# Attention block on one core: the far tiles of the transposed probabilities turned by VectorE in 32x32 blocks and put together by sixteen transfers a unit

## The chip, the cores and the metric

The kernel runs on one core of a Trainium2 chip. The metric is the time of one execution on the device in microseconds (us). The engines are TensorE (PE in the profile, its weight loads PEld), VectorE (DVE), ScalarE (ACT), GpSimd (POOL) and SyncE (SP), which here only issues DMA transfers. SBUF is the on-chip memory, PSUM the memory that TensorE writes its products to. Each engine works through its own queue in order; semaphores order the engines among each other.

## The reference

Two attention layers with layer norms between them and a mixture of experts at the end, for 2 batches of 1024 rows of 256. The part that the change touches is the second attention, 16 heads of 128:

```python
q = q * cos + _rotate_half(q) * sin
k = k * cos + _rotate_half(k) * sin
scores = jnp.einsum('bhqd,bhkd->bhqk', q, k) / math.sqrt(HD)
scores = jnp.where(causal[None, None], scores, jnp.finfo(jnp.float32).min)
probs = jax.nn.softmax(scores.astype(jnp.float32), axis=-1).astype(q.dtype)
out = jnp.einsum('bhqk,bhkd->bhqd', probs, v)
out = out.transpose(0, 2, 1, 3).reshape(b, s, H * HD)
return out @ wo + bo
```

## The kernel before

The work is cut into 34 units: units 0 and 1 are the first attention of the two batches, units 2 to 33 one head of one batch each (`unit_of`; a pair of heads is four units, and `r` in the code is the unit's place in its pair). The 1024 rows of a unit are 8 tiles of 128 queries. Every product is done three times, with operands split into a high part (fp32r) and a low part (the rest): ScalarE writes the high part (`high_...`), VectorE or GpSimd subtracts it (`low_...`), and `product` on TensorE multiplies high by high, high by low and low by high.

For a unit u the steps are: `project_q(u, x)` for x = 0 to 3 (queries and keys of 512 rows each); `add_bias` (ScalarE), `swap` (SP, two transfers of 128 KB that exchange the halves of 64 partitions), `rotate` (VectorE), `turn` (GpSimd, two operations), `high_qk`, `low_qk` (GpSimd); `scores(u, i)` for tile i, its causal width (i + 1) x 128; `row_max` (VectorE, which also adds the mask); `exponent` (ScalarE, into `prob_s` for tiles 0 to 3 and into the two halves of `prob_b` in turn for tiles 4 to 7); `transposes(u, i)` on TensorE, one for each 128 keys, through two PSUM banks `ps_t`; `high_p` and `low_p`, which write the transposed probabilities as `pT_hi` and `pT_lo`; `outputs(u, c)` for the 512 queries of half c; `high_o`, `low_o`; `out_project(u, c, g)`; and `accumulate` on VectorE. `project_v` makes the values of a pair of heads, half of them in each unit.

For tiles 4 to 7 the transposes come in two groups (`TG`): 4 far tiles (keys 0 to 511, all of them visible) and i - 3 near tiles (keys 512 to 1023, up to the diagonal). A unit has 10 transposes for tiles 0 to 3 and 16 far and 10 near ones for tiles 4 to 7.

The order is written out by hand, as one list for each engine, `head(u)`, in the middle of which n = u + 1 stands for the next unit: its projections and rotations are done beside the exponents of unit u. `head` runs for u = 3 to 30; `start` and `ends` hold the orders of the first and the last units. The products on TensorE that aren't scores or transposes take the two banks `ps_m` in turn (`take_bank`): a product waits until the contents of the bank from two uses before have been read. `work` (`qb`, `qs`, `qc`) holds the queries and keys on their way through the rotation, `rows` and `hf` are used by the layer norms alone.

## Time and profile before

| | us |
|---|---|
| runs before, median of 3 (lowest to highest) | 1116.94 (1116.71 to 1118.32) |
| profiled execution, from the first to the last instruction | 1115.4 |
| TensorE busy | 1105.2 |
| VectorE busy | 834.9 |
| ScalarE busy | 748.3 |
| GpSimd busy | 638.1 |
| queue of SP, share of the 16 DMA engines' span | 19.9% |

The profiled execution's span leaves out what lies around the first and last instruction. TensorE's busy time is the union of its records, and its records overlap. A row of a timeline gives the start and the length of an instruction; where an engine works without a gap, the distance from one start to the next is what an instruction costs it.

### The profile page before, as it was taken

The numbers are of one execution on the slowest core, as the hardware profiler recorded it, in microseconds if no ns is written. First come the engines' busy times: TensorE is split into PE (matmuls) and PEld (weight loads), VectorE is DVE, ScalarE is ACT, GpSimd is POOL, SyncE is SP. The second block draws the span as 40 slices with busy tenths as digits, with TensorE's granted clock in tenths as the row PEclk, the third lists the DMA queues.
The fourth block names the chain that finished last, engine by engine and source line by source line (L and its number), as shares of the span: only waits on it lengthen the run. The fifth ranks groups of instructions, "written<-read, shape, count | busy, mean of one in ns | idle before, by whom it ended". The sixth has DMA issues, their size and how long they took to land.

```text
span 1115.4 us, 20396 instructions
## 1 busy us (share of the span) xinstructions
PE 1105.2 (99%) x7100; PEld 1006.7 (90%) x7100; DVE 834.9 (75%) x1978; ACT 748.3 (67%) x1584; POOL 638.1 (57%) x516
## 2 busy tenths in 40 slices
PE   9999999999999999999999999999999999999997
PEld 8999899999999999999999999999999999988897
DVE  7776777777777777777777777777777777977776
ACT  5666867666666666666666666666666666688765
POOL 2217666555555555555555555555555556777676
PEclk9999999999999999999999999999999999999999
DMA  5002412121212121212121212121211212230102
GB/s 176 1 1 62 129 39 53 39 62 39 52 39 62 39 53 39 60 39 50 37 60 39 52 39 62 39 48 44 62 38 37 50 40 57 48 110 14 39 1 76
DMA packets 33285, 56.54 MB, mean 51 GB/s; under 512 B 5792, under 2 KB 10016, under 8 KB 33184
## 3 DMA queue, kind: packets, MB, share of 16 engines
q1 hardware_dynamic: 33040, 55.21, 19.9%
q8 instruction: 57, 0.93, 0.3%
q14 instruction: 44, 0.36, 0.1%
q10 hardware_dynamic: 144, 0.03, 0.0%
HBM read 17.47 MB, written 4.19 MB: 19 GB/s over the span
## 4 chain that ended last, share of the span: by engine, by line
PE 95%; POOL 2%; issue 1%; ACT 1%; DMA 1%; DVE 1%; SPq 0%; POOLq 0%; ACTq 0%; DVEq 0%
PE ps_m L458 58%; PE ps_s L458 23%; PE ps_t L608 12%; PE ps_m L505 1%; DMA work<-in_attn_w 0%; POOL acc L2341 0%; POOL qk_lo L2346 0%; PE ps_m L479 0%; POOL wqk_lo L2346 0%; PE ps_t L458 0%; POOL pT_lo L2354 0%; DMA work<-work 0%; POOL acc L2330 0%; PE ps_m L666 0%; PE ps_m L667 0%
## 5 line engine op out<-in xcount | busy, mean ns | idle before, releaser
L2296 POOL TENSOR_TENSOR work<-work,rope 128x512 f32<-128x512 f32 x128 | 165.5, 1293 | 222.8 <-DMA work<-work 222.7
L1784 DVE TENSOR_TENSOR pT_lo<-ps_t,pT_hi 128x512 fp32r<-128x512 f32 (+3 forms) x408 | 210.8, 551 | 32.7 <-ACT pT_hi L1201 30.2
L1201 ACT ACTIVATE pT_hi<-ps_t 128x512 fp32r<-128x512 f32 (+3 forms) x408 | 182.8, 489 | 65.3 <-PE ps_t L608 65.1
L1777 DVE CUSTOM_DVE_ANT_0 ps_s<-ps_s,causal 128x128 f32<-128x128 f32 (+7 forms) x272 | 203.5, 767 | 6.7 <-PE ps_s L458 4.1
L2300 POOL TENSOR_TENSOR work<-work 128x512 f32<-128x512 f32 x128 | 167.6, 1310 | 10.0
L2307 POOL TENSOR_TENSOR qk_lo<-work,qk_hi 128x512 fp32r<-128x512 f32 x128 | 163.0, 1293 | 17.8 <-ACT qk_hi L1158 17.8
L1152 ACT ACTIVATE work<-ps_m,bqk 128x512 f32<-128x512 f32 x128 | 88.8, 694 | 116.5 <-PE ps_m L458 116.4
L1817 DVE SCALAR_TENSOR_TENSOR acc<-ps_m,rinv,acc 128x256 f32<-128x256 f32 x272 | 118.6, 478 | 63.0 <-PE ps_m L458 61.7
L1194 ACT ACTIVATE prob_b<-ps_s,nmax 128x640 f32<-128x640 f32 (+3 forms) x136 | 130.3, 958 | 17.9 <-DVE nmax L1777 14.6
L458 PE MATMUL ps_s<-qk_hi 128*128 128x384 f32 (+5 forms) x384 | 140.6, 366 | 0.0
L1738 DVE SCALAR_TENSOR_TENSOR work<-ps_m,bqk,rope 128x512 f32<-128x512 f32 x128 | 95.5, 746 | 54.3 <-ACT work L1152 54.0
L458 PE MATMUL ps_m<-pT_lo,v_hi 128*128 128x512 f32 (+3 forms) x384 | 132.6, 345 | 0.0
L458 PE MATMUL ps_m<-pT_hi,v_lo 128*128 128x512 f32 (+3 forms) x384 | 132.6, 345 | 0.0
L458 PE MATMUL ps_s<-qk_lo,qk_hi 128*128 128x384 f32 (+5 forms) x384 | 131.5, 343 | 0.0
L458 PE MATMUL ps_s<-qk_hi,qk_lo 128*128 128x384 f32 (+5 forms) x384 | 130.9, 341 | 0.0
L458 PE MATMUL ps_m<-pT_hi,v_hi 128*128 128x512 f32 (+3 forms) x384 | 130.1, 339 | 0.0
L608 PE MATMUL ps_t<-ident,prob_b 128*128 128x128 f32 x884 | 120.1, 274 | 0.4 <-DVE pT_lo L1784 0.4
L608 PEld LDWEIGHTS ps_t<-ident,prob_b 128*128 128x128 f32 x884 | 99.7, 140 | 9.8 <-issue 1.2
L458 PE MATMUL ps_m<-hT_hi,wqk_hi 128*128 128x512 f32 x256 | 103.6, 405 | 0.0
L1158 ACT ACTIVATE qk_hi<-work 128x512 fp32r<-128x512 f32 x128 | 79.1, 641 | 36.4 <-POOL work L2300 36.3
L458 PE MATMUL ps_m<-hT_lo,wqk_hi 128*128 128x512 f32 x256 | 101.0, 395 | 0.0
L458 PE MATMUL ps_m<-hT_hi,wqk_lo 128*128 128x512 f32 x256 | 100.5, 393 | 0.0
(235 smaller groups left out, 2822.7 us busy)
## 6 DMA issues: line engine op xcount, KB each, us to landing
work<-work SPq DMA_DIRECT2D x256, 128.0 KB, 2.3
wst<-in_head_qk SPq DMA_DIRECT2D x16, 256.0 KB, 2.9
acc<-in_x_tiles SPq DMA_DIRECT2D x8, 256.0 KB, 6.8
wo_st<-in_L_ffn_wo SPq DMA_DIRECT2D x16, 128.0 KB, 2.4
wst<-in_pair_v SPq DMA_DIRECT2D x8, 256.0 KB, 3.0
x_rows<-acc SPq DMA_DIRECT2D x4, 512.0 KB, 3.6
wst<-in_expert SPq DMA_DIRECT2D x8, 256.0 KB, 3.0
rope<-x_rows SPq DMA_DIRECT2D x4, 512.0 KB, 4.1
```

The lines of the kernel that those rows point to most:

```text
L458: ins = pe.matmul(out, lhs[x], rhs[y], start=first and k == 0, stop=last and k == 2)
L608: last = pe.transpose(t_bank(u, i, j)[:, k * P:(k + 1) * P], probs(i)[:, part], ident[:, :])
L1152: act.activation(qb[:, x % 2, :], m_bank("q", u, x), ACT.Identity, bias=bqk[:, j, head_:head_ + 1]).then_inc(qb_done.sem, qb_done.up(u, x))
L1194: act.activation(probs(i), all_scores[:, score_range(i)], ACT.Exp, bias=nmax[:, u % 2, i:i + 1], scale=-1.0, accum_out=rsum[:, u % 2, i:i ...
L1201: act.activation(pT_hi[:, slots, cols], t_bank(u, i, j)[:, 0:size * P].rearrange("p (j q) -> p j q", q=P), ACT.Copy).then_inc(t_hi.sem, t_ ...
L1738: dve.scalar_tensor_tensor(qc[:, ring3(u, x), :], m_bank("q", u, x), bqk[:, j, head_:head_ + 1], cos_t[:, c * CH:(c + 1) * CH], ALU.add, A ...
L1777: dve.tensor_tensor_reduce(s, s, causal[:, T - (i + 1) * P:T], -1.0, ABOVE_ALL, ALU.add, ALU.min, accum_out=nmax[:, u % 2, i:i + 1]).then_ ...
L1784: dve.tensor_tensor(pT_lo[:, slots, cols], t_bank(u, i, j)[:, 0:size * P].rearrange("p (j q) -> p j q", q=P), pT_hi[:, slots, cols].bitcas ...
L1817: last = dve.scalar_tensor_tensor(acc[:, b, tile, :], src[:, t * D:(t + 1) * D], rinv[:, u % 2, tile:tile + 1], acc[:, b, tile, :], ALU.mu ...
L2296: pool.tensor_tensor(qs[:, x % 2, :], qs[:, x % 2, :], sin_t[:, c * CH:(c + 1) * CH], ALU.mult).then_inc(sin_done.sem, sin_done.up(u, x))
L2300: pool.tensor_tensor(qc[:, ring3(u, x), :], qc[:, ring3(u, x), :], qs[:, x % 2, :], ALU.add).then_inc(rope_done.sem, rope_done.up(u, x))
L2307: pool.tensor_tensor(qk_lo[:, u % 2, j, cols], qc[:, ring3(u, x), :], qk_hi[:, u % 2, j, cols].bitcast(F32), ALU.subtract).then_inc(qk_lo_ ...
```

## The change

For the units 3 to 30 (`FAR_UNITS`) the 16 far transposes leave TensorE. VectorE turns each tile's 512 far keys in blocks of 32x32 into a buffer `turned` (`turn_far`, four operations a unit). It takes the place of `rows` and `hf`. A block transpose leaves every block in its own 32 partitions; so sixteen transfers of 32 partitions x 512 elements, 64 KB each, put the blocks where the product needs them: `exchange(u)` on SP issues 8 of them and `exchange(u)` on ScalarE the other 8, each once the fourth `turn_far` is done and the near product of the first half has been read out of `pT`. They land in the slots 0 to 3 of `pT_lo`, keys in order. `high_far` (ScalarE) then rounds two slots' worth at a time into `pT_hi`, `low_far` (VectorE) subtracts it in place, both from SBUF to SBUF with 1024 columns in an operation, two a unit. Since the queries of a tile come in four groups of 32 that way, the near tiles are written in the same order of queries (`by_quarter`), and `high_o` and `low_o` put them back. `outputs(u, 1)` becomes `near_outputs(u)` and two times `far_outputs(u, k)`, near first, with the columns and the number of products as before. `exponent` waits in addition for `turn_far` on the half of `prob_b` that it writes over, and `turn_far(u, 4)` for both queues' transfers of the unit before.

```diff
+FAR_UNITS = range(3, LAST - 2)
+FAR = 4 * CH
+Q4 = 32
...
+def groups_of(u, i):
+
+    return [(1, i - 3)] if is_far(u) and i >= 4 else list(enumerate(TG[i]))
...
-        rows = sb("rows", [P, TC, D])
-        hf = sb("hf", [P, KD, CH])
+        shared_ln = sb("shared_ln", [P, FAR])
+        rows = shared_ln[:, 0:TC * D].rearrange("p (t d) -> p t d", d=D)
+        hf = shared_ln[:, TC * D:FAR].rearrange("p (k n) -> p k n", n=CH)
+        turned = shared_ln[:, :].rearrange("p (g m i q) -> p g m i q", g=4, m=4, i=4)
+        turned_by_keys = shared_ln[:, :].rearrange("p (g n) -> p g n", g=4)
...
+            def far_outputs(u, k):
...
+                pe.wait_ge(far_lo.sem, far_lo.at(u, k))
...
+                for j in (2 * k, 2 * k + 1):
+                    high, low = (x[:, 0:4, j * P:(j + 1) * P] for x in (pT_hi, pT_lo))
+                    last = product(out, (v_hi[:, s, j, vals], v_lo[:, s, j, vals]), (high, low), False, j == TC - 1)
...
+            def high_far(u, k):
+                act.wait_ge(exchanged.sem, exchanged.at(u))
+                act.wait_ge(exchanged_act.sem, exchanged_act.at(u))
+                act.activation(far_part(pT_hi, k), far_part(pT_lo, k).bitcast(F32),
+                               ACT.Copy).then_inc(far_hi.sem, far_hi.up(u, k))
+
+            def exchange(u):
+                act.wait_ge(turn_done.sem, turn_done.at(u, NT - 1))
+                act.wait_ge(pv_mm.sem, pv_mm.at(u, 0))
+                for g in (2, 3):
+                    for k in range(4):
+                        act.dma_start(pT_lo[k * Q4:(k + 1) * Q4, g, :].bitcast(F32),
+                                     turned_by_keys[g * Q4:(g + 1) * Q4, k, :]).then_inc(exchanged_act.sem, 16)
+                exchanged_act.up(u)
...
+            def turn_far(u, i):
+                dve.wait_ge(exp_done.sem, exp_done.at(u, i))
...
+                dve.transpose(out=turned[:, :, :, i - 4, :].rearrange("p g m q -> p m g q"),
+                              in_=prob_b[:, i % 2, 0:CH].rearrange("p (m g k) -> p m g k", g=4, k=Q4)).then_inc(turn_done.sem, turn_done.up(u, i))
+
+            def low_far(u, k):
+                dve.wait_ge(far_hi.sem, far_hi.at(u, k))
+                dve.tensor_tensor(far_part(pT_lo, k), far_part(pT_lo, k).bitcast(F32), far_part(pT_hi, k).bitcast(F32),
+                                  ALU.subtract).then_inc(far_lo.sem, far_lo.up(u, k))
...
                 swap(n, 1)
+                exchange(u)
                 swap(n, 2)
```

The lists of `head(u)` are written in another order. TensorE's new list in full:

```
T(u,0) T(u,1) project_q(n,0) out_project(u-1,1,0) T(u,2) T(u,3) scores(u,4) scores(u,5)
project_q(n,1) out_project(u-1,1,1) T(u,4) scores(u,6) scores(u,7) outputs(u,0) T(u,5)
project_q(n,2) project_q(n,3) T(u,6) T(u,7) out_project(u,0,0) scores(n,0) scores(n,1)
scores(n,2) out_project(u,0,1) project_v project_v scores(n,3) near_outputs(u)
far_outputs(u,0) far_outputs(u,1)                         (T is transposes)
```

The three engines whose order the prediction speaks of, first ScalarE, from the second half of a unit to the first exponents of the next. `pT_hi<-ps_t` is a copy of transposed probabilities, `work<-ps_m` is add_bias, `prob_s` and `prob_b` are exponents. Before:

```order
L1194 ACTIVATE prob_b,rsum<-ps_s,nmax 128x1024 [waits t_mm,max_done]
L1201 ACTIVATE pT_hi<-ps_t 128x4x128 [waits t_mm]
L1201 ACTIVATE pT_hi<-ps_t 128x3x128 [waits t_mm]
L1163 ACTIVATE v_hi<-ps_m 128x512 [waits v_mm]
L1201 ACTIVATE pT_hi<-ps_t 128x4x128 [waits t_mm] x2
```

and now:

```order
L1269 ACTIVATE pT_hi<-ps_t 128x12x32 [waits t_mm]
L1218 ACTIVATE work<-ps_m,bqk 128x512 [waits swapped_1,qk_mm]
L1269 ACTIVATE pT_hi<-ps_t 128x16x32 [waits t_mm]
L1283 DMA pT_lo<-shared_ln 32x512 [waits pv_mm,turn_done]
L1283 DMA pT_lo<-shared_ln 32x512 x7
L1229 ACTIVATE v_hi<-ps_m 128x512 [waits v_mm]
L1275 ACTIVATE pT_hi<-pT_lo 128x4x256 [waits exchanged_act,exchanged] x2
L1263 ACTIVATE prob_s,rsum<-ps_s,nmax 128x128 [waits t_mm,max_done]
```

Behind the last near copies stand the eight issues, then the values, and then the two large copies that wait for both queues' transfers; the next unit's exponents moved behind those.

VectorE, in the middle of a unit, around the low part of the first half's output (`oT_lo`). Before:

```order
L1777 ISA ps_s,nmax<-ps_s,causal 128x896 [waits s_mm]
L1777 ISA nmax 128x1
L1795 RECIPROCAL rinv<-rsum 128x4 [waits exp_done]
L1790 TENSOR_TENSOR oT_lo<-ps_m,oT_hi 128x512 [waits o_hi]
L1784 TENSOR_TENSOR pT_lo<-ps_t,pT_hi 128x4x128 [waits t_hi]
```

and now:

```order
L1861 ISA ps_s,nmax<-ps_s,causal 128x1024 [waits s_mm]
L1861 ISA nmax 128x1
L1878 STREAM_TRANSPOSE shared_ln<-prob_b 128x4x4x32 [waits exp_done]
L1888 TENSOR_TENSOR oT_lo<-ps_m,oT_hi 128x512 [waits o_hi]
L1878 STREAM_TRANSPOSE shared_ln<-prob_b 128x4x4x32 [waits exp_done]
L1867 TENSOR_TENSOR pT_lo<-ps_t,pT_hi 128x8x32 [waits t_hi]
```

The first transpose there is tile 6, the second tile 7; `oT_lo`, on which project_q(n, 3) waits for its bank, stands behind the row maximum of tile 7 and the transpose of tile 6. Before, it stood right behind the row maximum of tile 6.

TensorE, at the end of a unit: the second half's product, whose first row is a far tile and which ends with the near tiles of 512, 384, 256 and 128 columns; two steps of three are left out. Before:

```order
L458 MATMUL ps_m<-pT_hi,v_hi 128x512 [waits t_lo,v_lo_done]
...
L458 MATMUL ps_m<-pT_hi,v_hi 128x512 [waits t_lo]
...
L458 MATMUL ps_m<-pT_hi,v_hi 128x384
...
L458 MATMUL ps_m<-pT_hi,v_hi 128x256
...
L458 MATMUL ps_m<-pT_hi,v_hi 128x128
```

and now:

```order
L499 MATMUL ps_m<-pT_hi,v_hi 128x512 [waits t_lo,v_lo_done]
...
L499 MATMUL ps_m<-pT_hi,v_hi 128x4x96
...
L499 MATMUL ps_m<-pT_hi,v_hi 128x4x64
...
L499 MATMUL ps_m<-pT_hi,v_hi 128x4x32
...
L499 MATMUL ps_m<-pT_hi,v_hi 128x512 [waits far_lo]
...
L499 MATMUL ps_m<-pT_hi,v_hi 128x512 [waits far_lo]
...
L649 MATMUL ps_t<-ident,prob_s 128x128 [waits t_lo,exp_done] x2
```

The near product comes first now, and each half of the far product waits for its own `low_far`.

## Rows read from the trace of the kernel before

**Rows 1.** The page: busy time of each engine, and the chain that ended last

```profile
PE 1105.2 (99%) x7100; PEld 1006.7 (90%) x7100; DVE 834.9 (75%) x1978; ACT 748.3 (67%) x1584; POOL 638.1 (57%) x516
...
PE 95%; POOL 2%; issue 1%; ACT 1%; DMA 1%; DVE 1%; SPq 0%; POOLq 0%; ACTq 0%; DVEq 0%
```

**Rows 2.** Busy time by stretch of eight units; then TensorE's clock, DMA share, GB/s

```profile
core 0: us, PE busy (x) PEld busy (x) DVE busy (x) ACT busy (x) POOL busy (x), PEclk, DMA share, GB/s
278.42:504.65 226.23, 226.21 (x1442) 206.23 (x1441) 169.01 (x377) 149.87 (x331) 128.54 (x103) 1.00 0.21 47
504.65:730.71 226.06, 226.06 (x1442) 206.35 (x1441) 169.30 (x377) 149.87 (x331) 128.54 (x103) 1.00 0.21 48
```

**Rows 3.** Timeline of TensorE: start us, length us, engine, line, operation, tiles

```profile
503.05 1.03 PE L608 MATMUL ps_t<-ident,prob_b 128*128 128x128 f32 x8
...
503.84 0.38 PE L458 MATMUL ps_m<-wv_hi,hT_hi 128*128 128x256 f32 x1
...
506.06 0.40 PE L458 MATMUL ps_m<-pT_hi,v_hi 128*128 128x512 f32 x1
506.29 0.39 PE L458 MATMUL ps_m<-pT_lo,v_hi 128*128 128x512 f32 x1
...
511.12 0.42 PE L458 MATMUL ps_s<-qk_hi 128*128 128x384 f32 x1
...
511.38 0.33 PE L458 MATMUL ps_s<-qk_lo,qk_hi 128*128 128x384 f32 x1
511.55 0.34 PE L458 MATMUL ps_s<-qk_hi,qk_lo 128*128 128x384 f32 x1
```

**Rows 4.** Groups by line and shape, ScalarE and VectorE: busy us, mean ns; a timeline pair

```profile
L1201 ACT ACTIVATE pT_hi<-ps_t 128x512 fp32r<-128x512 f32 x171 | 98.6, 595 | 28.5 <-PE ps_t L608 28.5
L1030 ACT ACTIVATE acc<-acc 128x1024 f32<-128x1024 f32 x1 | 1.1, 1078 | 0.0
...
L1784 DVE TENSOR_TENSOR pT_lo<-ps_t,pT_hi 128x512 fp32r<-128x512 f32 x170 | 114.2, 685 | 23.1 <-ACT pT_hi L1201 23.1
L1777 DVE CUSTOM_DVE_ANT_0 ps_s<-ps_s,causal 128x1024 f32<-128x1024 f32 x29 | 35.5, 1223 | 0.0
L1624 DVE CAST hT_hi<-hf 128x256 fp32r<-128x256 f32 x2 | 0.6, 288 | 0.0
...
557.76 0.98 ACT L1201 ACTIVATE pT_hi<-ps_t 128x512 fp32r<-128x512 f32 x2 [0.18 <-PE ps_t L608]
558.62 0.60 ACT L1163 ACTIVATE v_hi<-ps_m 128x512 fp32r<-128x512 f32 x1
```

**Rows 5.** DMA issues (timeline; us to landing by form) and what a swap moved

```profile
0.74 0.41 ACTq L1025 DMA_DIRECT2D vec<-in_vectors  x1
...
0.74 0.39 SPq L2520 DMA_DIRECT2D acc<-in_x_tiles  x1
1.18 0.42 SPq L2523 DMA_DIRECT2D work<-in_attn_w  x1
...
231.74 0.46 SPq L2555 DMA_DIRECT2D work<-work  x1
232.25 0.59 SPq L2556 DMA_DIRECT2D work<-work  x1
232.89 0.58 SPq L2535 DMA_DIRECT2D wst<-in_head_qk  x1
233.51 0.45 SPq L2540 DMA_DIRECT2D wst<-in_pair_v  x1
...
work<-work SPq DMA_DIRECT2D x256, 128.0 KB, 2.3
wst<-in_head_qk SPq DMA_DIRECT2D x16, 256.0 KB, 2.9
out_rows<-prob_b SPq DMA_DIRECT2D x2, 128.0 KB, 1.7
...
501.00:501.50 0.50, 0.50 (x7) 0.50 (x6) 0.24 (x2) 0.33 (x3) 0.50 (x1) 1.00 0.94 197
501.50:502.00 0.50, 0.50 (x6) 0.50 (x5) 0.03 (x1) 0.50 (x2) 0.41 (x1) 1.00 1.02 221
```

**Rows 6.** Timeline: VectorE's operation with both inputs in SBUF, and GpSimd beside it

```profile
227.04 0.66 DVE L1751 SCALAR_TENSOR_TENSOR wqk_lo<-wst,wqk_hi 128x512 fp32r<-128x512 f32 x1
...
517.78 1.29 POOL L2296 TENSOR_TENSOR work<-work,rope 128x512 f32<-128x512 f32 x1
518.13 1.48 DVE L1751 SCALAR_TENSOR_TENSOR wqk_lo<-wst,wqk_hi 128x512 fp32r<-128x512 f32 x1
519.14 1.62 POOL L2300 TENSOR_TENSOR work<-work 128x512 f32<-128x512 f32 x1
```

200 lines of the change are left out of this document (130 added, 70 removed).

## The prediction

> **What bounds the kernel now.** Three views in this order. First the table of busy time and the chain that ended last [rows 1]: TensorE is busy 1105.2 of 1115.4 us and carries 95% of the chain, VectorE 75%, ScalarE 67%, GpSimd 57%. Then the busy times of a stretch of eight units [rows 2]: 226.23 us, 28.28 us a unit (the next eight 226.06, 28.26), TensorE without a gap at full clock, VectorE 21.1 and ScalarE 18.7 us a unit. The 28 units from 3 to 30, which the change touches, are 28 x 28.26 = 791 us of the span. So only TensorE's own work counts there today, and nothing that another engine does until it makes TensorE wait. Third the timelines of the engines around a unit, for prices and for the order in which things wait.
>
> TensorE's prices are distances between starts, since its records overlap. Eight transposes start at 503.05 and the next product at 503.84: 0.10 us each, although a record lasts 0.27. Products of 512 columns start 0.23 apart [rows 3].
>
> **Taken away on TensorE.** Of the 36 transposes of a unit the 16 far ones go: 1.6 us. Where a product follows transposes its first step is stretched by about 0.1 (0.26 instead of 0.17 us for 384 columns, [rows 3]); eight such places become five, 0.3 us. The products keep their columns. TensorE's own work falls from 28.26 to about 26.4 us a unit; all of it over 28 units would be 53 us.
>
> **Moved to others.** VectorE loses four subtractions of 512 columns from PSUM (0.69 each, [rows 4]), and gets four block transposes of 512 and two subtractions of 1024 columns with both inputs in SBUF. No transpose of VectorE is in the trace. Below stands the conversion of 256 columns at 0.29, which doubled is some 0.45; above the two-input operation held up to 1.48 us [rows 6]; I take the 0.69 of the plain 512-column form, as it reads and writes as many columns. The 1024-column subtractions I put at 1.2, like the row maximum of 1024 [rows 4]. VectorE comes to 21.1 - 2.7 + 2.8 + 2.4 = 23.6 us a unit. ScalarE loses four copies of 512 (0.60), gets two of 1024 (1.08, [rows 4]) and eight DMA issues: 18.7 - 2.4 + 2.2 + 4.5 = 23.0. SP issued eight DMAs a unit and mostly waited; it now issues sixteen. None of the three reaches 26.4 by its sum, so the question is the chain of one exchange.
>
> **The price of an issue.** A single swap issue on SP lasts 0.46 us, one right behind it 0.59, and four in a row start at 231.74, 232.25, 232.89 and 233.51, 0.59 apart; the first ones of the kernel start 0.47 apart, and the one issue on ScalarE lasts 0.41 [rows 5]. The eighth issue thus starts 3.3 to 4.4 us behind the first; I take 3.9 (0.56 apart), between the short and the long spacing. ScalarE can do nothing else for some 4.5 us. A swap's two transfers moved 197 to 221 GB/s while in flight [rows 5], so 64 KB is 0.3 us of transfer: issuing, not moving, sets the pace. The Trainium skill (DMA: Bandwidth & Descriptors, Issuing engines are not separate DMA queues) says that issuing from several engines only saves sequencer time, usually small beside the transfer. By the rows it is larger; were it small, as that page has it, the sum below would shrink by about 1.5 us a unit. That is the first rival.
>
> **The sum for one unit,** from the first transpose on TensorE (0). Up to the end of the near product `outputs(u, 0)` TensorE has 23,040 columns (10.25 us at 0.23 per 512), 11 transposes and three changes: 11.7. project_q(n, 3) needs the bank that this product leaves, so the high part (0.2 + 0.60 on ScalarE) and the low part (0.69 on VectorE, behind row_max(u, 7) and turn_far(u, 6)); it starts at 13.6 instead of 13.4 and ends at 15.0. The three transposes of tile 6 end at 15.4. ScalarE does high_p(u, 6), add_bias(n, 3) and high_p(u, 7) behind them, starts 0.43 to 0.6 apart [rows 4], and issues its first transfer at **17.1**. SP, which waits for the last block transpose alone, starts about 14.5 and is done first, so ScalarE's half decides: the last issue at 21.0 (+3.9); landed at 23.2 (+2.2: the swaps' median from issue to landing is 2.3 for 128 KB, [rows 5]; 1.7 is the shortest of any form there, 2.9 to 3.0 that of loads of 256 KB); high_far(u, 0) done at 24.3 (+1.1); low_far(u, 0) at 26.0 (+1.2, and +0.5 for the wait below); low_far(u, 1) at 27.7 (the same again), while TensorE finishes the first far product; the second far product 1.4: **29.1**.
>
> The 0.5: the trace has one operation of VectorE with both inputs in SBUF in the units, L1751. It lasts 0.66 with GpSimd idle and 1.48 at 518.13, where GpSimd is in an operation from 517.78 and the next one, begun at 519.14, is itself stretched to 1.62 [rows 6]. So the two hold each other. low_far is such an operation, and at that time GpSimd is in its densest stretch, six operations of 1.29 us for (n, 2) and (n, 3), whose swaps SP now issues behind the exchange. The wait is 0 to 1.3 for each of the two; I take 0.5, somewhat under the mean of 0.65.
>
> What TensorE has meanwhile: from 15.4 the last transposes, out_project, scores, project_v and near_outputs, about 7.9 us with the waits for banks, so it stands from about 23.5 to 26.1 and again for a moment ahead of the second far product. The late ScalarE work, exponent(n, 3) and high_o(u, 1), delays out_project(u, 1, 0) in the next unit by 0 to 0.3 us; I leave it at 0.
>
> Result: 29.1 - 28.26 = +0.84 us a unit, over 28 units +23.5 us. The profiled execution is 1115.4 us from first to last instruction, the median of three runs 1116.94, 1.5 us more, and that holds for both kernels: 1116.9 + 23.5 = **1140 us**. The units outside 3 to 30 keep their order.
>
> **Bounds.** Cheapest: the exchange starts at 16.6, issues 3.3, landing 1.7, no wait for GpSimd, block transposes at 0.45: 16.6 + 3.3 + 1.7 + 1.1 + 1.2 + 2.8 = 26.7, near TensorE's own 26.4. Dearest: 17.9 (block transposes of 1.3) + 4.4 + 3.2 + 1.1 + 2.5 + 2.5 + 1.4 = 33.0. Neither end has all its terms at once with much chance.
>
> **Rivals.**
> (A) Faster: issuing on ScalarE is cheap. Place: exchange(u) in ScalarE's queue. The gain and loss meet where 29.1 becomes 28.26, so at seven spacings of 0.44 instead of 0.56. If ScalarE's sequencer issues while its last copies still run (exchange at 16.6) and at 0.42 a piece, as its only row has it, the unit is 16.6 + 2.9 + 2.2 + 1.1 + 1.7 + 1.7 + 1.4 = 27.6: -18 us, 1098. For it: that row of 0.41. Against it: every string of issues in the trace. 0.20. The same with no wait for GpSimd and everything hidden, 26.4 to 26.7 us a unit, 1064 to 1073: 0.05.
> (B) The gains and the new wait cancel within 0.2%, 28.18 to 28.34 us a unit: 0.05.
> (C) Slower by more: GpSimd takes the port between the two low_far each time. Then the second starts 1.3 us late and not 0.5, the first up to 1.3 too: 29.1 + 1.6 = 30.7, +68 us, 1185. For it: GpSimd's next operation did follow at once at 519.14. Partly so, +0.8 us a unit, would be 1163. 0.15 together.
> (D) The two queues hinder each other: ScalarE's issues run into SP's last ones and into the swaps (n, 2) and (n, 3) behind them, some six issues of 0.5 us; waiting for them adds up to 3 us: 32, 1220. Against it: at 0.74 us both queues started an issue together, and each took its 0.4 us [rows 5]. The Trainium skill (Perfetto Trace Analysis, DMA Instruction — HWDGE) says the opposite, that the descriptor generator is shared by the sequencers and locked while one uses it; by the rows nothing is added. 0.05.
> The change does what it says: the order on the engines shows the 16 transposes gone and the sixteen transfers there.
>
> **Chances.** Forecast (28.34 to 30.0 us a unit) 0.50, A 0.25 in all, B 0.05, C 0.15, D 0.05. The range from 1095 to 1178 holds the forecast, B, A without its far end and the partial C. A measurement of this kernel can tell about 0.2% (2.2 us) from no change: faster 0.25, same 0.05, slower 0.70.
>
> **What would show it.** In the changed profile: units of 29.1 us; TensorE's busy share down and its longest waits on pT_lo of low_far; eight issues on ScalarE 0.56 apart from 17.1 in the unit, landing about 2.2 behind the last; low_far of 1.2 to 2.5 us beside GpSimd. I am wrong if TensorE stays near 99% (A), if the wait ahead of the far products is mainly on GpSimd's account (C), or if issues on either queue last over 1 us (D). A block transpose of much over 0.7 us would move the wait to project_q(n, 3).

## The result and the profile after the change

The changed kernel takes **1279.2 us** (median; 1276.5 to 1286.9), the kernel before 1117.6 in the same comparison: a ratio of 1.146, 95% interval 1.142 to 1.149. The forecast was 1140 with a range up to 1178: the sign was right, the size was not. The difference of 162 us is 5.8 us for each of the 28 units, where 0.84 was forecast.

The page of the changed kernel, its busy times and its chain, stands against [rows 1]: TensorE falls from 1105.2 us in a span of 1115.4 to 1133.4 in 1279.1, and from 95% of the chain to 51%. VectorE (19%), ScalarE's DMA queue (ACTq, 10%), DMA (7%) and ScalarE come in.

```profile
span 1279.1 us, 20088 instructions
...
PE 1133.4 (89%) x6652; PEld 981.6 (77%) x6652; DVE 955.4 (75%) x2034; ACT 734.9 (57%) x1528; POOL 688.7 (54%) x516
...
PE 51%; DVE 19%; ACTq 10%; DMA 7%; ACT 6%; issue 5%; POOL 2%; SPq 0%; POOLq 0%; DVEq 0%
```

The busy times of eight units (columns as in [rows 2]) show where to look: 270.60 us, 33.8 a unit instead of 28.26, TensorE without work for 35.8 us of them, 4.5 a unit, and a granted clock of 0.94 instead of 1.00. Its busy time, 234.78, is no less than the 226.21 of before, though 16 transposes a unit are gone: where the clock falls, the same products take longer. (How much, the run with all three changes shows below.)

```profile
core 0: us, PE busy (x) PEld busy (x) DVE busy (x) ACT busy (x) POOL busy (x), PEclk, DMA share, GB/s
311.30:581.90 270.60, 234.78 (x1314) 200.46 (x1313) 201.50 (x392) 145.76 (x313) 142.50 (x103) 0.94 0.30 71
```

The list of what TensorE waits for (total us, times, longest) names three places: low_far (L1883), the exponents (prob_b), and the low part of the values (v_lo), which frees the bank that the near product writes.

```profile
PE ps_m L499 <- DVE pT_lo L1883: 60.7, 43, 2.3
PE ps_t L649 <- ACT prob_b L1263: 32.5, 14, 3.3
PE ps_m L499 <- DVE v_lo L1829: 27.5, 28, 2.1
```

**One unit followed along its chain** (an r = 2 unit; its first transpose on TensorE is at 581.88). ScalarE's timeline: the first of its eight issues is at 599.10, 17.2 us in, 17.1 was forecast. The eight last until 604.13, and high_far starts at 606.28.

```profile
598.99 0.68 ACT L1218 ACTIVATE work<-ps_m,bqk 128x512 f32<-128x512 f32 x1
599.10 0.52 ACTq L1283 DMA_DIRECT2D pT_lo<-shared_ln  x1
599.56 0.60 ACT L1269 ACTIVATE pT_hi<-ps_t 128x512 fp32r<-128x512 f32 x1
599.65 4.48 ACTq L1283 DMA_DIRECT2D pT_lo<-shared_ln  x7
604.18 0.60 ACT L1229 ACTIVATE v_hi<-ps_m 128x512 fp32r<-128x512 f32 x1 [4.02 <-issue]
606.28 2.00 ACT L1275 ACTIVATE pT_hi<-pT_lo 128x1024 fp32r<-128x1024 f32 x2 [1.50 <-DMA pT_lo<-shared_ln]
```

VectorE: the last block transpose takes 0.71 (0.69 was forecast); both low_far together 4.09, and GpSimd's two operations beside them 2.15 and 2.27 instead of 1.29 (first fence VectorE, second GpSimd).

```profile
596.70 0.71 DVE L1878 STREAM_TRANSPOSE shared_ln<-prob_b 128x512 f32<-128x512 f32 x1 [0.18 <-ACT prob_b L1263]
...
607.37 4.09 DVE L1883 TENSOR_TENSOR pT_lo<-pT_lo,pT_hi 128x1024 fp32r<-128x1024 f32 x2 [1.87 <-ACT pT_hi L1275]
```
```profile
606.86 1.29 POOL L2400 TENSOR_TENSOR work<-work,rope 128x512 f32<-128x512 f32 x1 [7.46 <-DMA work<-work]
608.23 2.15 POOL L2404 TENSOR_TENSOR work<-work 128x512 f32<-128x512 f32 x1
610.34 2.27 POOL L2400 TENSOR_TENSOR work<-work,rope 128x512 f32<-128x512 f32 x1
```

On TensorE the near product ends at 607.7; the far products wait for low_far:

```profile
609.28 0.50 PE L499 MATMUL ps_m<-pT_hi,v_hi 128*128 128x512 f32 x1 [1.60 <-DVE pT_lo L1883]
611.52 0.50 PE L499 MATMUL ps_m<-pT_hi,v_hi 128*128 128x512 f32 x1 [0.57 <-DVE pT_lo L1883]
```

The next unit begins at 613.01. This unit lasts 31.1 us, so the forecast's chain is the right one and 2.0 us short in it: 0.1 up to the first issue, 1.1 from there to high_far, 0.7 in the two low_far, the rest behind them.

**The next unit, r = 3, is another matter.** From the timelines of ScalarE and, in the last row, TensorE:

```profile
615.54 0.64 ACT L1236 ACTIVATE wqk_hi<-wst 128x512 fp32r<-128x512 f32 x1
620.97 0.42 ACT L1251 ACTIVATE wo_hi<-wo_st 128x256 fp32r<-128x256 f32 x1 [4.79 <-PE ps_m L499]
621.30 0.96 ACT L1269 ACTIVATE pT_hi<-ps_t 128x384 fp32r<-128x384 f32 x2
623.19 0.79 ACT L1263 ACTIVATE prob_b<-ps_s,nmax 128x640 f32<-128x640 f32 x1 [0.93 <-DVE nmax L1861]
...
624.13 0.33 PE L649 MATMUL ps_t<-ident,prob_b 128*128 128x128 f32 x1 [3.25 <-ACT prob_b L1263]
```

high_o_weights (L1251) stands 4.79 us for the last product of `out_project(u - 1, 1, 1)`, which reads the weights that it overwrites, and high_p(u, 2), high_p(u, 3) and exponent(u, 4) stand behind it in ScalarE's queue. TensorE then stands 3.25 us ahead of `transposes(u, 4)`. The changed order had put that step at the unit's start; before, it stood at the end. The other half of the weights, `high_o_weights(p, 1)` in the r = 0 units, kept its place, but exponent(u, 4) moved behind it. In the kernel before, the r = 3 copy waited for nothing and the r = 0 copy up to 1.4 us, 9.8 us in all; in the changed kernel both wait, 56.1 us in 14 times. From the timeline of before:

```profile
335.36 0.42 ACT L1185 ACTIVATE wo_hi<-wo_st 128x256 fp32r<-128x256 f32 x1
347.52 0.42 ACT L1185 ACTIVATE wo_hi<-wo_st 128x256 fp32r<-128x256 f32 x1 [1.40 <-PE ps_m L458]
```

The prediction does not speak of these steps.

Over all 28 units, from the timelines of TensorE, ScalarE and VectorE, the chain's terms are (means, in us; the columns on the right are kernels from the experiments below):

| term | forecast | changed | both weight steps late | and swap(n, 2) first | and swap(n, 3) inside |
|---|---|---|---|---|---|
| first transpose to ScalarE's first issue | 17.1 | 18.31 | 16.59 | 16.60 | 16.36 |
| first issue to start of high_far | 6.1 | 8.25 | 8.14 | 7.45 | 8.13 |
| high_far to low_far | 1.1 | 1.09 | 1.09 | 1.09 | 1.09 |
| the two low_far | 3.4 | 4.22 | 4.24 | 3.64 | 2.36 |
| end of low_far to the next unit | 1.4 | 2.16 | 2.07 | 1.75 | 2.00 |
| unit | 29.1 | 34.02 | 32.14 | 30.54 | 29.95 |
| time of the kernel | 1140 | 1279.2 | 1225.5 | 1177.6 | 1166.6 |

### The profile page after: what moved, and what is told of

It reads as the page before. It is cut to its first block, busy times and chain, and to the rows that moved or that the text cites. A ratio compares the mean times of both kernels' runs of the same rounds, so it can differ in the third digit from the quotient of the medians.

```text
span 1279.1 us, 20088 instructions
## 1 busy us (share of the span) xinstructions
PE 1133.4 (89%) x6652; PEld 981.6 (77%) x6652; DVE 955.4 (75%) x2034; ACT 734.9 (57%) x1528; POOL 688.7 (54%) x516
## 4 chain that ended last, share of the span: by engine, by line
PE 51%; DVE 19%; ACTq 10%; DMA 7%; ACT 6%; issue 5%; POOL 2%; SPq 0%; POOLq 0%; DVEq 0%
PE ps_m L499 32%; PE ps_s L499 12%; ACTq L1283 10%; DVE pT_lo L1883 7%; DMA pT_lo<-shared_ln 6%; PE ps_t L649 5%; DVE ps_s L1861 4%; ACT pT_hi L1275 2%; DVE shared_ln L1878 2%; ACT pT_hi L1269 2%; DVE acc L1915 1%; DVE pT_lo L1867 1%; DVE work L1822 1%; DVE oT_lo L1888 1%; DVE wqk_lo L1835 1%
## 5 line engine op out<-in xcount | busy, mean ns | idle before, releaser
L2400 POOL TENSOR_TENSOR work<-work,rope 128x512 f32<-128x512 f32 x128 | 193.0, 1508 | 338.5 <-DMA work<-work 338.5
L499 PE MATMUL ps_m<-pT_hi,v_hi 128*128 128x512 f32 (+3 forms) x384 | 150.6, 392 | 93.2 <-DVE pT_lo L1883 60.7
L2404 POOL TENSOR_TENSOR work<-work 128x512 f32<-128x512 f32 x128 | 189.4, 1480 | 10.0
L1867 DVE TENSOR_TENSOR pT_lo<-ps_t,pT_hi 128x512 fp32r<-128x512 f32 (+3 forms) x296 | 142.7, 492 | 58.0 <-ACT pT_hi L1269 57.8
L499 PEld LDWEIGHTS ps_m<-pT_hi,v_hi 128*128 128x128 f32 x384 | 78.9, 205 | 134.1 <-DVE pT_lo L1883 74.6
L1883 DVE TENSOR_TENSOR pT_lo<-pT_lo,pT_hi 128x1024 fp32r<-128x1024 f32 x56 | 118.1, 2147 | 59.6 <-ACT pT_hi L1275 59.6
L1269 ACT ACTIVATE pT_hi<-ps_t 128x512 fp32r<-128x512 f32 (+3 forms) x296 | 125.3, 451 | 39.7 <-PE ps_t L649 39.4
L499 PE MATMUL ps_m<-pT_lo,v_hi 128*128 128x512 f32 (+3 forms) x384 | 143.2, 373 | 0.0
L1229 ACT ACTIVATE v_hi<-ps_m 128x512 fp32r<-128x512 f32 x72 | 42.9, 596 | 143.8 <-PE ps_m L499 82.4
L1263 ACT ACTIVATE prob_s<-ps_s,nmax 128x128 f32<-128x128 f32 (+3 forms) x136 | 70.9, 524 | 66.8 <-DVE nmax L1861 66.6
```

Of the source, the lines that this page charges most:

```text
L499: ins = pe.matmul(out, lhs[x], rhs[y], start=first and k == 0, stop=last and k == 2)
L1263: act.activation(probs(i), all_scores[:, score_range(i)], ACT.Exp, bias=nmax[:, u % 2, i:i + 1], scale=-1.0, accum_out=rsum[:, u % 2, i:i ...
L1269: act.activation(transposed(pT_hi, u, i, j), t_tiles(u, i, j), ACT.Copy).then_inc(t_hi.sem, t_hi.up(u, i, j))
L1867: dve.tensor_tensor(transposed(pT_lo, u, i, j), t_tiles(u, i, j), transposed(pT_hi, u, i, j).bitcast(F32), ALU.subtract).then_inc(t_lo.sem ...
L1883: dve.tensor_tensor(far_part(pT_lo, k), far_part(pT_lo, k).bitcast(F32), far_part(pT_hi, k).bitcast(F32), ALU.subtract).then_inc(far_lo.se ...
L2400: pool.tensor_tensor(qs[:, x % 2, :], qs[:, x % 2, :], sin_t[:, c * CH:(c + 1) * CH], ALU.mult).then_inc(sin_done.sem, sin_done.up(u, x))
```

## Experiments

Times are medians; the kernel before gave 1116.6 to 1117.0 beside all of them.

### The weight steps on ScalarE

```diff
                 if r == 3:
                     high_qk_weights(p + 1, 1)
-                    high_o_weights(p + 1, 0)
                 high_p(u, 2)
 ...
                 high_p(u, 4)
+                if r == 3:
+                    high_o_weights(p + 1, 0)
                 exponent(u, 6)
```

> One step moved: on ScalarE high_o_weights(p + 1, 0) goes from ahead of high_p(u, 2) to behind high_p(u, 4); nothing is left out. In the trace of the changed kernel ScalarE stands 4.8 us ahead of the first half of this step in each of the 7 units that have it (56.1 us in 14 waits on out_project's last product), and high_p(u, 2) and high_p(u, 3) stand behind it; TensorE waits up to 3.3 us for them and later for prob_b (32.5 us in all), and the units with this step last some 37 us, those behind them 34, the others 31 to 33. Theory W (the moved weight step costs on its own): the 7 long units fall to the length of the others, 4 to 7 us each, so 1279 - 28 to 49 = 1230 to 1251. Rival E (the exchange's chain sets each unit, the stall only takes its place): at most 1 us a unit, 1272 to 1279.

Measured: 1240.1, ratio 1.109 (1.106 to 1.112). Theory W: 39 us from the place of one copy. ScalarE's first issue in the seven r = 3 units comes at 16.4 us on the mean instead of 20.9. In the r = 0 units it stays at 19.1, and ScalarE's waits still show a wait of that step, 24.7 us in 7 times; that is the other half of the weights, `high_o_weights(p, 1)`. So that was moved as well:

```diff
-                if r == 0:
-                    high_o_weights(p, 1)
                 exponent(u, 4)
 ...
                 high_p(u, 4)
+                if r == 0:
+                    high_o_weights(p, 1)
```

> Both steps on the output weights stand behind high_p(u, 4) on ScalarE: high_o_weights(p + 1, 0) of the r = 3 units and high_o_weights(p, 1) of the r = 0 units (the kernel of 1240 had moved the first alone). Nothing is left out. In the changed kernel's trace ScalarE's first issue comes 16.0 and 17.1 us behind the unit's first transpose in r = 1 and r = 2 units, 20 to 22 in r = 3 and 19.2 in r = 0; with the first step late the r = 0 units stay at 19.0. Theory W (the second step is the same stall): the r = 0 units come to 16.0 to 16.5, 2.5 to 3 us in each of 7: 1240 - 21 = 1219, 1212 to 1225. Rival V (the r = 0 units are late through add_value_bias(p, 1) on VectorE): 1236 to 1244.

Measured: 1225.5, ratio 1.097 (1.095 to 1.099), 15 us less where 21 were expected, at the upper end of theory W: the mechanism holds (ScalarE no longer waits ahead of L1251, the first issue comes at 16.59 on the mean), the gain is somewhat smaller. Together the two steps cost 54 us.

### The number of transfers

```diff
-                    for k in range(4):
+                    for k in (0,):
                         act.dma_start(pT_lo[k * Q4:(k + 1) * Q4, g, :].bitcast(F32),
```
(and the same on SP)

> Leaves out 12 of the 16 transfers of each exchange, so that three quarters of the far tiles are old data: SP issues 2 and ScalarE 2. Everything else, the waits too, is as in the changed kernel. Theory I (the string of issues sets the chain): ScalarE's last issue comes 6 x 0.65 = 3.9 us sooner, and the landing behind it, 2.7 in the trace, falls to 2.0 or so; 3.9 to 4.5 us a unit while the chain is late, down to TensorE's own 26.4: 33.7 - 4.5 = 29.2, 28 x 4.5 = 126, so 1153 to 1170, with the stall of the weight step still in it. Rival P (a fixed time from the first issue to the landing, or the order of the steps, holds the units): less than 1.5 us a unit, 1237 or above. Rival Q (the queues hinder each other, so that fewer transfers free SP too): more than 5 us a unit, under 1140.

Measured: 1171.4, ratio 1.048 (1.047 to 1.050): 108 us less, 3.9 a unit. Theory I, 1.4 us above its range: from the first issue to high_far it takes 4.8 us instead of 8.2. TensorE's waits show low_far almost gone (4.3 us instead of 60.7), those on v_lo down (10.2 instead of 27.5) and the wait of the weight step untouched (32.1); the granted clock is 0.984 instead of 0.964. So the 108 us are what the late chain cost in all above TensorE's own work and the waits of the weight steps, not the price of twelve issues by themselves.

### GpSimd beside low_far

```diff
+                w_ = 16 if is_far(u - 1) else CH
-                pool.tensor_tensor(qs[:, x % 2, :], qs[:, x % 2, :], sin_t[:, c * CH:(c + 1) * CH],
+                pool.tensor_tensor(qs[:, x % 2, 0:w_], qs[:, x % 2, 0:w_], sin_t[:, c * CH:c * CH + w_],
```
(and so in the other two steps)

> GpSimd's three steps of the rotation (L2398 to L2404 and the subtraction behind it) work on 16 columns instead of 512 in the units behind a unit with an exchange; the rest of their columns is left out. VectorE and all waits stay. In the trace of the changed kernel the two low_far last 2.15 us each while GpSimd works, 4.1 to 4.6 for both, and GpSimd's operations beside them 2.15 to 2.27 instead of 1.5. Theory G (the two engines hold each other): low_far falls to 1.2 each, 2 us a unit, and the rotation ends sooner: 1279 - 28 x 2 = 1223, 1210 to 1235. Rival V (a subtraction with both inputs in SBUF in this form lasts 2.1 by itself): low_far stays at 2.0 to 2.2 and the time within 1265 to 1279.

Measured: 1206.7, ratio 1.081 (1.078 to 1.084): 72 us less, more than theory G asked for. The rows of low_far, first in the changed kernel, then here (shortest, median and longest in ns):

```profile
L1883 DVE TENSOR_TENSOR pT_lo<-pT_lo,pT_hi x56: 1337/2294/2325, 170.5 to 1087.4; 128x1024 fp32r<-128x1024 f32 x56
```
```profile
L1883 DVE TENSOR_TENSOR pT_lo<-pT_lo,pT_hi x56: 1215/1226/1242, 168.0 to 1019.5; 128x1024 fp32r<-128x1024 f32 x56
```

All 56 last 1.22 to 1.24 with GpSimd nearly idle, the 1.2 of the sum; beside GpSimd 46 of the 56 last 2.2 to 2.3. Rival V is out. The hold itself is 52 us of the 72 (28 x 1.84, from 4.22 for the pair to 2.38). The rest is spread: by the timelines 0.3 us a unit ahead of the first issue, 0.1 from there to high_far and 0.2 behind low_far, at a clock of 0.984 instead of 0.964. What makes the first part is not shown; GpSimd's rotation ends sooner there too.

### Do the costs add, and what is TensorE's own work?

> The late weight step and the small GpSimd steps together (GpSimd's rotation works on 16 of 512 columns in the units behind an exchange; the rest is left out). Alone they gave 1240 and 1207, 39 and 72 us under the changed kernel. Theory S (two separate costs on the path of different units or places): they add, 1279 - 39 - 72 = 1168; 1158 to 1178. Rival T (they overlap): 1185 to 1205. What is left above 1117 is then the exchange's chain with the forecast's own prices: issue, landing, high_far, low_far 1.23, second far product.

Measured: 1175.1, ratio 1.051 (1.049 to 1.054): 104 of the 111 us that the two gave apart. They add nearly.

> The late weight step, the small GpSimd steps, and 4 of 16 transfers, together (12 transfers and most of GpSimd's rotation are left out). Sum of the three savings: 39 + 108 + 72 = 219, 1060. Theory F (TensorE's own work is 26.4 us a unit, as forecast): the units can't become shorter than 26.4, so 1117 - 28 x 1.86 = 1065 at best, 1065 to 1085. Rival O (the order of the steps has waits of its own): units above 27.5, over 1095.

Measured: 1096.9, ratio 0.982 (0.981 to 0.984), above theory F and at the lower edge of rival O. The three gave 219 us apart and 182 together. The units last 27.6 us on the mean. A stretch of 226 us there has TensorE busy for 221.10 (columns as above):

```profile
400.00:626.00 226.00, 221.10 (x1345) 195.97 (x1344) 190.91 (x404) 150.37 (x323) 31.16 (x106) 1.00 0.23 57
```

So its own work is 27.6 x 0.978 = 27.0 us a unit, near the 26.4 of the forecast, and the order has 0.6 us of small waits besides; the second weight step is still among them (24.4 us of ScalarE's waits, 9.4 of TensorE's on prob_b). Own work of 27.0 would have been worth 28 x 1.26 = 35 us, not 53, and this run, with most of the exchange and the rotation left out, gets 20 of them.

It also gives a size to the fall of the clock. From the start of the second exchange unit to the end of the last, 27 units, TensorE is busy in the changed kernel and here (first row and second):

```profile
175.68:1096.47 920.79, 789.80 (x4436) 671.47 (x4434) 688.91 (x1326) 494.77 (x1065) 485.17 (x347) 0.95 0.29 70
170.70:916.32 745.62, 727.82 (x4435) 645.72 (x4434) 625.22 (x1326) 493.70 (x1063) 97.20 (x346) 1.00 0.24 58
```

That is 29.3 and 27.0 us a unit for the same products: of the 6.5 us by which the units differ, 2.3 are products that take longer, and 4.2 are TensorE without work. How much of the 2.3 lies on the chain and how much beside it is not separated.

### The order of the change with the transposes back on TensorE

```diff
-FAR_UNITS = range(3, LAST - 2)
+FAR_UNITS = range(0)
 ...
-                transposes(u, 4)
                 scores(u, 6)
                 scores(u, 7)
                 outputs(u, 0)
+                transposes(u, 4)
                 transposes(u, 5)
```
(the block transposes, the exchange, high_far and low_far go; on ScalarE high_qk(n, 0) and high_o(u, 0), on VectorE row_max(u, 7) and low_o(u, 0) stand ahead of high_p(u, 4) and low_p(u, 4))

> The changed kernel's order of steps on all engines, but the far tiles are transposed by TensorE as before, without block transposes, exchange, high_far and low_far; transposes(u, 4) stands behind outputs(u, 0), since it writes what that product reads. Nothing is left out. Theory O1 (order harmless except for the weight step): TensorE has its 28.26 us a unit again and stands only in the units with the weight step, 3 to 7 us in each of 7: 1117 + 21 to 49 = 1138 to 1166. Rival O2 (the order itself, with exponent(u, 4) late and the late rotations, makes TensorE wait in each unit): over 1 us more a unit, 1180 to 1230. Rival O3 (the weight step's stall comes only together with the exchange): 1117 to 1130.

Measured: 1273.7, ratio 1.140 (1.139 to 1.142), worse than any theory had it. Its waits say why, and that it is no clean test:

```profile
PE ps_t L649 <- DVE pT_lo L1862: 76.2, 57, 1.5
PE ps_s L499 <- ACT prob_b L1261: 32.1, 14, 3.3
PE ps_m L499 <- DVE v_lo L1824: 10.5, 7, 2.1
```

The second row is the weight step. The first is new: with all transposes in it, `transposes(u, 4)` to `transposes(u, 7)` stand so close that each waits for a transpose bank to be emptied, a wait that the changed kernel does not have. It suggests that the new order works only with the far tiles gone; how much of the 162 us the order costs in the changed kernel it does not show.

### TensorE's clock

```diff
                 near_outputs(u)
+                fill(20)
                 far_outputs(u, 0)
```

> Twenty matmuls of 128 columns whose result nobody reads stand on TensorE between the near product and the first far product (some 2 us at 0.10 us each); nothing is left out. In the trace of the changed kernel's relative with the late weight step, TensorE stands 2.21 us ahead of the first far product and 0.35 ahead of the second, and the products of 512 columns of the second then start 0.42 us apart instead of 0.23: half the clock for some 2.5 us, 1.1 to 1.2 us a unit. Theory K (the idle time itself makes the clock fall, and this is a cost of its own): the granted clock rises from 0.964 to 0.98 or more, the second far product goes at 0.23 a step, and 28 x 1.0 = 28 us go, 1245 to 1260. Rival N (the clock falls for another reason, or the chain through low_far hides it): within 1270 to 1285. Rival M (the added work itself delays the far products): slower, up to 28 x 0.7 = 20 us, 1299.

Measured: 1302.3, ratio 1.166 (1.162 to 1.170): rival M, by my own mis-sizing. The twenty matmuls last 4.68 us and not 2:

```profile
552.79 0.28 PE L499 MATMUL ps_m<-pT_hi,v_lo 128*128 128x128 f32 x1
552.91 4.68 PE L706 MATMUL ps_t<-ident 128*128 128x128 f32 x40
557.34 0.49 PE L499 MATMUL ps_m<-pT_hi,v_hi 128*128 128x512 f32 x1
```

low_far(u, 0) was ready about two microseconds before they ended. The granted clock did rise to 0.986, and both far products ran at 0.23 a step. The fall of the clock is best seen in the kernel with the first weight step late, where TensorE stood 2.21 and 0.35 us:

```profile
563.25 0.50 PE L499 MATMUL ps_m<-pT_hi,v_hi 128*128 128x512 f32 x1 [2.21 <-DVE pT_lo L1884]
563.59 0.39 PE L499 MATMUL ps_m<-pT_lo,v_hi 128*128 128x512 f32 x1
...
565.48 0.79 PE L499 MATMUL ps_m<-pT_hi,v_hi 128*128 128x512 f32 x1 [0.35 <-DVE pT_lo L1884]
566.08 0.63 PE L499 MATMUL ps_m<-pT_lo,v_hi 128*128 128x512 f32 x1
566.50 0.63 PE L499 MATMUL ps_m<-pT_hi,v_lo 128*128 128x512 f32 x1
566.93 0.63 PE L499 MATMUL ps_m<-pT_hi,v_hi 128*128 128x512 f32 x1
```

The first far product steps 0.23 to 0.34 apart, the second 0.42, which is the lower of the two levels (1.2 GHz). Not every stand does this: in the unit shown above, behind 1.60 and 0.57 us, all steps stay at 0.23. With the stand filled by matmuls the clock is back at 0.986, so it does follow the standing; what it costs on the chain by itself is not separated.

### Which queue issues what

```diff
-                for g in (2, 3):
+                for g in (3,):
                     for k in range(4):
                         act.dma_start(
 ...
-                for g in (0, 1):
+                for g in (0, 1, 2):
                     for k in range(4):
                         sp.dma_start(
```

> The kernel with the late weight step (1240), but SP issues 12 of the 16 transfers and ScalarE 4; nothing is left out. In the trace SP starts its string at 15.4 us in the unit and ScalarE at 17.1. Theory L (the last landing alone sets the unit, as in the prediction's sum): SP's last issue starts at 15.4 + 11 x 0.62 = 22.2 against ScalarE's 21.5 before, and its landing is 2.1 against 2.7: the unit keeps its length within 0.2 us, 1234 to 1246. Theory Q (ScalarE's blocked queue is a cost of its own: high_values, v_lo and the exponents behind it): ScalarE is free 2.5 us sooner, and the unit falls by 1 us or more, under 1215. Rival R (SP's later swaps (n, 2) and (n, 3) hold the next unit): 1255 or more.

Measured: 1252.5, ratio 1.121 (1.119 to 1.123), 12 us more than with eight and eight, between theory L and rival R. From ScalarE's first issue to high_far it takes 8.16 us against 8.22, as theory L has it, with SP's string now ending 3.8 us behind ScalarE's; but the first issue itself comes at 18.1 on the mean instead of 17.2. Freeing ScalarE earlier takes the waits on v_lo away (1.4 us in all) and brings nothing, since those on low_far rise to 73.4. The swaps, now behind twelve transfers, cost a little (10.5 us of waits on qk_lo where there were 2.9): rival R in small.

### The swaps ahead of the exchange

The hold of low_far was so far shown by leaving work out. This moves one step of SP:

```diff
                 swap(n, 1)
+                swap(n, 2)
                 exchange(u)
-                swap(n, 2)
                 swap(n, 3)
```

> As the run before, and SP issues swap(n, 2) ahead of its eight transfers instead of behind them. Nothing is left out. Theory G (low_far is held by GpSimd's work on (n, 2) and (n, 3)): GpSimd does (n, 2) before the landing, at most (n, 3) is left beside low_far; the two low_far fall from 4.2 us towards 3, 1 us a unit, and SP's string starts at most 0.5 later, which isn't the last: 28 x 1.0 = 28 us, 1185 to 1205. Rival S (SP's delay or the longer queue eats it): 1210 to 1225.

Measured: 1177.6, ratio 1.054 (1.052 to 1.056): **48 us less than with both weight steps late, by the place of one swap**, more than theory G said. The table shows three terms that fall: the landing (8.14 to 7.45 from first issue to high_far), the two low_far (4.24 to 3.64) and the end (2.07 to 1.75, at a clock of 0.995 instead of 0.975). In the changed kernel SP issues both swaps, four transfers, right behind its string, while ScalarE's last ones are still in flight (first fence); here one swap stands ahead of the string and only the other behind it (second fence, the third has ScalarE):

```profile
603.25 0.55 SPq L2659 DMA_DIRECT2D work<-work  x1
603.84 0.60 SPq L2660 DMA_DIRECT2D work<-work  x1
604.54 0.54 SPq L2659 DMA_DIRECT2D work<-work  x1
```
```profile
494.69 0.46 SPq L2660 DMA_DIRECT2D work<-work  x1
495.19 0.60 SPq L2661 DMA_DIRECT2D work<-work  x1
495.89 5.00 SPq L2669 DMA_DIRECT2D pT_lo<-shared_ln  x8
500.98 0.56 SPq L2660 DMA_DIRECT2D work<-work  x1
```
```profile
496.55 4.68 ACTq L1283 DMA_DIRECT2D pT_lo<-shared_ln  x7
502.72 2.01 ACT L1275 ACTIVATE pT_hi<-pT_lo 128x1024 fp32r<-128x1024 f32 x2 [0.84 <-DMA pT_lo<-shared_ln]
```

From the end of ScalarE's string (501.23) to high_far it is 1.49 us here, 1.7 on the mean; in the changed kernel it is 2.15 in the unit shown and 2.4 on the mean. Still one swap, (n, 3), stands behind. Putting it between SP's fourth and fifth transfer:

```diff
-                for g in (0, 1):
-                    for k in range(4):
+                for m, (g, k) in enumerate([(0, 0), (0, 1), (0, 2), (0, 3), (1, 0), (1, 1), (1, 2), (1, 3)]):
+                    if m == 4:
+                        swap(u + 1, 3)
 ...
                 exchange(u)
-                swap(n, 3)
```

> As the run of 1178 (both weight steps late, swap(n, 2) ahead of SP's transfers), and swap(n, 3) between SP's fourth and fifth transfer instead of behind the eighth. Nothing is left out. There the time from the end of ScalarE's last issue to high_far fell from 2.45 to 1.70 us and the two low_far from 4.24 to 3.64, with no other change than the place of one swap. Theory G (what is left of the hold is GpSimd's work on (n, 3)): the two low_far come to 2.4 to 3.0, and the landing stays at 1.7; 0.6 to 1.2 us a unit, 1178 - 17 to 34 = 1144 to 1161. Rival S (SP's string now ends behind ScalarE's, 15.4 + 5.0 + 1.2 = 21.6 us against 21.7, and its landing is last): 1170 to 1185.

Measured: 1166.6, ratio 1.044 (1.043 to 1.046), 11 us less, between theory G, whose range ends at 1161, and rival S. The hold is gone entirely, with nothing left out:

```profile
L1883 DVE TENSOR_TENSOR pT_lo<-pT_lo,pT_hi x56: 1212/1222/1272, 167.6 to 973.4; 128x1024 fp32r<-128x1024 f32 x56
```

but SP's string now ends 0.9 us behind ScalarE's and gives back 0.7 us of the landing.

### The far products in the next unit

If the chain of 29 to 30 us is the bound, the far products can be closed over more of TensorE's work:

```diff
                 transposes(u, 1)
                 project_q(n, 0)
-                out_project(u - 1, 1, 0)
-                transposes(u, 2)
-                transposes(u, 3)
+                if is_far(u - 1):
+                    far_outputs(u - 1, 0)
+                    far_outputs(u - 1, 1)
                 scores(u, 4)
                 scores(u, 5)
+                transposes(u, 2)
+                out_project(u - 1, 1, 0)
+                transposes(u, 3)
 ...
                 near_outputs(u)
-                far_outputs(u, 0)
-                far_outputs(u, 1)
+                if not is_far(n):
+                    far_outputs(u, 0)
+                    far_outputs(u, 1)
 ...
```

> The exchange stays whole, but the far products of a unit stand in the next unit on TensorE, behind transposes(u, 0), transposes(u, 1) and project_q(n, 0), and high_o(u, 1), low_o(u, 1), high_p(n, 0) and high_p(n, 1) behind them; the weight step stands late. ScalarE takes the exponents of the next unit ahead of high_far. Nothing is left out. TensorE has 2 us more of its own work (0.2 + 1.8) before it needs low_far(u, 0). Theory H (the exchange's chain of some 31 us is the only bound): the chain is closed over 2 us more of work, 31.1 - 2.0 = 29.1 or less, and without the idle time the clock stays up (1 us more): 28 to 29 us a unit, 1110 to 1140. Rival Z (the swaps (n, 2) and (n, 3), which SP issues behind the exchange, then hold scores(u, 4) by their rotation): 29.5 to 31, 1150 to 1195.

Measured: 1245.5, ratio 1.115 (1.113 to 1.116): above both theories' ranges, and no better than the 1240 without the move. TensorE waited 66.9 us for v_lo, which stands behind the issues and high_far on ScalarE. The next two tried to free it:

> The far products in the next unit as in the run before (1245), with 12 transfers on SP and 4 on ScalarE, and both high_values of the unit ahead of high_far on ScalarE; nothing is left out. In that run's trace TensorE waits 66.9 us for v_lo and 39.0 for low_far: v_hi of the unit stands behind ScalarE's eight issues and behind high_far. Theory Q (ScalarE's queue): the waits on v_lo fall under 15 us, and the units to 28 to 29: 1110 to 1140. Rival L (the landing of the last transfer and two low_far of 2.2): waits on low_far take their place, 1190 to 1240.

> As the run before, but all 16 transfers are issued by SP, with swap(n, 2) ahead of them and swap(n, 3) behind; ScalarE issues none; nothing is left out. SP's string then lasts 16 x 0.6 = 9.6 us and the last transfer lands some 27.5 to 28.5 us behind the unit's first transpose; low_far(u, 1) is done some 5 us later. Theory L: TensorE waits for it each time, 33 us less the 2 us of work moved ahead: 31 us a unit, 1185 to 1205. Theory Q: since ScalarE is free, 1120 to 1160. Rival R (the rotation of (n, 3), issued behind the string, holds scores(u, 4)): 1200 or more, with waits on qk_lo.

Measured: 1339.8 (ratio 1.200, 1.198 to 1.203) and 1315.2 (1.177, 1.175 to 1.180), the first far above both theories, the second far above L and Q and in the open range of rival R. The wait on v_lo did go in both (none left, and 2.8 us). But in the first I had put high_qk(n, 2) ahead of high_far on ScalarE, and its rotation waits for a swap behind the exchange: ScalarE stood 158.7 us in all for it, and TensorE up to 7.8 us at a time for low_far. That run says nothing about the split. In the second the landing itself is late, the mechanism of theory L, though 110 us beyond its range: SP's string of sixteen lasts 10.06 us in one unit, ScalarE waits 124.9 us in all for the landing, and 30.4 us of waits on qk_lo come on top (rival R). With high_qk(n, 2) behind high_far, and then swap(n, 2) ahead of the exchange as well:

> The far products in the next unit, behind its first two transposes and project_q(n, 0), eight issues on each queue, both weight steps late, and on ScalarE both high_values and three exponents ahead of high_far, high_qk(n, 2) behind it (ahead of it in the run of 1340, where ScalarE stood 5.85 us for that rotation). Nothing is left out. Theory Q (v_hi behind the exchange was the wait): 28 to 29 us a unit, 1110 to 1140. Rival Z (the rotations of (n, 2) and (n, 3), late behind the exchange and slow beside low_far, hold scores(u, 4)): waits on qk_lo, 30 us or more, 1165 or above.

> The run before with swap(n, 2) ahead of SP's transfers. Nothing is left out. If both causes are as the runs so far say (weights, GpSimd beside low_far, far product at once behind the exchange), the unit comes to TensorE's own work, 27.5 us in the run of 1097 that left them all out: 1095 to 1117. Rival Z: (n, 3) alone still holds scores(u, 4), 1 to 2 us a unit: 1125 to 1155.

Measured: 1255.7 (1.124, 1.122 to 1.126), rival Z, with 58.3 us of waits on qk_lo; and 1191.1 (1.066, 1.065 to 1.068), above all ranges. Its waits are spread over four causes:

```profile
PE ps_m L499 <- DVE v_lo L1843: 32.0, 28, 2.4
PE ps_s L499 <- POOL qk_lo L2432: 22.9, 26, 2.6
PE ps_m L499 <- DVE oT_lo L1902: 20.1, 28, 1.7
PE ps_m L499 <- DVE pT_lo L1897: 10.2, 26, 0.6
```

> The far products in the next unit, both weight steps late, swap(n, 2) ahead of SP's transfers and swap(n, 3) between its fourth and fifth, SP 10 transfers and ScalarE 6. Nothing is left out. In the run of 1191 TensorE waited 32 us for v_lo, 23 for qk_lo, 20 for oT_lo and 10 for low_far. Theory Q: the first two and the last go, 1191 - 60 = 1131; 1120 to 1145. Rival: the waits move (low_far later by SP's two transfers more), 1160 to 1190. A time under 1117 would make the idea better than the kernel before; by these waits it stays above it.

Measured: 1196.0 (1.072, 1.070 to 1.074), the rival, 6 us above its range: v_lo falls to 8.8 and low_far rises to 45.8. Moving the far products is worth nothing here; every version of it is slower than the plain one with the same swaps and weight steps (1245.5 against 1240.1, 1255.7 against 1225.5, 1191.1 against 1177.6, 1196.0 against 1166.6). No version with the whole exchange came under 1116.7.

## Why the prediction was wrong, point by point

The mechanism was right and its sum too small. The steps that failed: the weight copies on ScalarE, put at nothing without a reason; the stretch from the first issue to high_far, 6.1 us in the sum and 8.25 measured; the wait of each low_far for GpSimd, 0.5 in the sum and 0.9 measured; and the clock, which the sum left out.

- **What bounds the kernel:** right. TensorE alone before; after, the chain of one exchange through ScalarE's half, in the forecast's order.
- **TensorE's own work, 26.4 us:** 27.0 measured, 0.6 above.
- **First issue at 17.1:** near for the units without a weight step (16.0 in r = 1, 17.1 in r = 2; 16.6 over all units once both steps were late, so 0.5 less than forecast), wrong for the other 14 (20.9 and 19.2). This is the step that was **left out**: the part on moved steps spoke of none of the weight steps. One of them had gone from the unit's end to its start, ahead of three things that TensorE needs, and the other stood ahead of exponent(u, 4) now. The two are worth 54 us, the second largest share of what was missing.
- **Issues 0.56 apart, landed 2.2 behind the last:** the term that was **mis-sized**. 6.1 us was the sum, 8.25 is the mean; 60 us over 28 units, the largest share. In 14 of 28 units the string of eight lasts 5.0 to 5.2 us, mostly 0.65 from start to start, at the upper end of the spacings in [rows 5] (0.63 where SP issues all sixteen alone, so the second queue is not the reason); in the other 14 it lasts 5.6 to 7.1, with one issue of over a microsecond in each. The spacing is 0.65 us of the excess, the long issues 0.65 on the mean, and the last landing 0.85: 3.0 behind the last start, 2.4 behind the end of the string, where 2.2 behind the last start was forecast. The median of all landings is 2.3, as it was in [rows 5], but the sum needs the last one. With one swap fewer behind SP's string that last landing takes 2.25; with none behind it, but SP's own string ending 0.9 us behind ScalarE's, 2.56. This points to what the other queue issues at the same time; which of it makes the landing late is not shown.
- **low_far 1.2 alone, and a hold of 0.5 each:** the price alone was exact (1.22 to 1.24), the block transpose too (0.70; its lower bound of 0.45 was a slip, since 0.29 doubled is 0.58, but only the cheapest end of the bounds used it). The hold was 0.9 each on the mean, and 1.0 to 1.1 in 46 of the 56. Rival C had the mechanism, and 0.15 of the chance was too little: the sentence that SP issues both swaps behind the exchange said already that GpSimd's work would start when the exchange lands. The two events follow from one, so they meet nearly each time and not by chance; a mean over chance meetings was the wrong figure. Moving the swaps, with nothing left out, took the hold away (4.24, 3.64, 2.36 for the pair), which shows it.
- **The end, 1.4:** 2.16 on the mean. In 13 units it is 1.54 to 1.58, at full clock; in 14 it is 2.1 to 2.8, with steps of the far products at half clock in most; in unit 30 it is 6.8, since the order behind it starts with other work, and that alone is 0.2 of the mean. The clock was not in the sum at all, although the sum itself had TensorE standing 2.6 us in each unit. In the last version the clock is up (0.996) and the end is still 2.00: with low_far at 1.2 the first far product isn't done when the second low_far is.
- **Rival A** fell: ScalarE does begin its issues while its last copies still run (599.10 beside the copy from 598.99), but no string was cheap. Of **rival D**, a part is there: the long issues. In the changed kernel ScalarE has 14 of over a microsecond (1.2 to 2.2 us), and each ends within 0.02 us of a long one of SP that began 0.3 to 0.5 us before or behind it (for instance 671.11 to 673.19 on ScalarE, 671.43 to 673.20 on SP). So something holds both queues at once and lets both go together. It isn't the other queue's issuing: with SP issuing all sixteen alone, issues of up to 1.99 us occur too, and the kernel before has ten of over a microsecond on SP in its whole run. The Trainium skill (Perfetto Trace Analysis, DMA Instruction — HWDGE) says that the descriptor generator is shared by the sequencers and locked while one uses it; two issues that end together do not look like one waiting for the other, so this trace does not show that lock. What the hold is stays open.
- **The signs named:** units of 29.1 (31.1 in the unit shown, 34.0 on the mean), the waits on pT_lo (there), TensorE's share down (there), 17.1 (there in half of the units), 0.56 (0.65).

Of the excess over the forecast, the terms of the table give 1.2 + 2.15 + 0 + 0.8 + 0.8 = 4.95 us a unit, 28 x 4.95 = 139 us, which is the whole of it. The first term is 1.7 for the weight steps less 0.5 that the forecast had too much.

## What to carry to other kernels

When a change reorders the queues, go through every step of the new order, also those that run only in one unit of four, and ask of each what it waits for and who stands behind it: a copy of weights that waits for the last reader cost nothing at the end of a unit here and up to 4.8 us of ScalarE's time at its start. When two things follow from one event (here the exchange: its landing starts high_far and low_far, and the swaps issued right behind it start GpSimd's rotation), price their collision as certain. And a step that is ended by the last of many transfers needs the time of the last one, beside whatever else is issued then, not the median; what may be issued ahead of the string should be.

## What the runs showed of the hardware

- A block transpose of 128x512 elements of four bytes on VectorE, in 32x32 blocks, takes 0.68 to 0.71 us, as long as a subtraction of that size from PSUM.
- VectorE's 128x1024 subtraction with both inputs in SBUF takes 1.22 us with GpSimd quiet and 2.29 beside its operations, which themselves go from 1.29 to 2.15 or more.
- Eight transfers of 64 KB issued in a row take 5.0 to 5.2 us of ScalarE in half of the cases and 5.6 to 7.1 in the others; single issues last up to 2.2 us. In the changed kernel each of ScalarE's 14 issues of over a microsecond ends within 0.02 us of a long one on SP.
- The last of sixteen such transfers landed 3.0 us behind the start of its issue with two swaps issued behind SP's string, 2.25 with one.
- 128-column products of two four-byte operands (fill) stand 0.22 us apart (4.68 us for 20, 40 records), transposes of the same size 0.10.
- TensorE's granted clock was 0.94 where it stood 4.5 us in a unit of 34, 1.00 before, and 0.996 in the version with swap(n, 3) inside SP's string, where it still stands up to 2.0 us at a time for low_far.
